# Second attention of a gated cross-attention block: where the softmax sums are inverted and how the values leave PSUM

## The reference, cut to what matters

```
q = LN(x) @ Wq.T + bq ; k, v = ctx @ Wk.T + bk, ctx @ Wv.T + bv      # 16 heads of 16
p = exp(clip(masked(q k / 4)))                                       # 16 x 128 x 128
attn = softmax over the context rows = p / sum(p)
delta = clip(residual_scale) * (concat_heads(attn @ v) @ Wo.T + bo)
x += tanh(g) * (LN(delta) * gamma + beta)
```

## Time and profile before

| | |
|---|---|
| median of 3 runs | 263.72 us (263.62 to 264.2) |
| profiled execution | 264.11 us, span 262.3 us |
| busy, share of the span | PE 81%, VectorE 69%, ScalarE 51%, GpSimd 32% |
| stage C, first product OT to last | 138.63 us to 190.57 us |
| granted TensorE clock, mean | 0.946 of full speed |

### The profile page before, as it was taken

The page is one execution under the profiler, slowest core; times in us unless marked ns, Lnnn a source line. Parts: engine busy times, 40 slices in busy tenths (PEclk is TensorE's granted clock), DMA queues, the critical chain, the costliest instruction groups (busy, mean ns, idle before and its releaser), DMA issues.

```text
span 262.3 us, 4538 instructions
## 1 busy us (share of the span) xinstructions
PE 212.0 (81%) x1658; PEld 174.5 (67%) x1658; DVE 181.0 (69%) x457; ACT 132.8 (51%) x296; POOL 83.9 (32%) x108
## 2 busy tenths in 40 slices
PE   0285557979889889897798688775999999999992
PEld 0264325858778778786576466654877888888882
DVE  2769879598988988786428999998984333262333
ACT  1138874478667667679755455553322323222220
POOL 2301111175856856868505333442100000000000
PEclk9999955699999999999959999997999999999999
DMA  5999003900000000000000000000000000020002
GB/s 169 369 390 301 5 0 139 343 1 0 2 0 0 2 1 0 2 2 0 0 2 2 0 2 4 0 4 0 2 2 0 0 0 2 0 80 2 0 0 80
DMA packets 9238, 12.55 MB, mean 48 GB/s; under 512 B 1025, under 2 KB 7937, under 8 KB 9217
## 3 DMA queue, kind: packets, MB, share of 16 engines
q1 hardware_dynamic: 8784, 12.07, 13.3%
q10 hardware_dynamic: 432, 0.20, 0.4%
HBM read 11.22 MB, written 1.05 MB: 47 GB/s over the span
## 4 chain that ended last, share of the span: by engine, by line
PE 50%; DVE 27%; ACT 7%; DMA 6%; issue 4%; POOL 3%; SPq 1%; DVEq 0%; ACTq 0%; POOLq 0%
PE PB L1259 16%; PE PB L1278 7%; DMA WRAW<-w_dram 6%; PE PB L1073 6%; PE PB L1172 4%; PE PB L1085 3%; DVE XV L524 3%; PE PB L1108 2%; PE PB L1112 2%; DVE HBQ L742 2%; PE PB L1019 2%; DVE RD L728 2%; DVE HBQ L572 2%; ACT SIL L906 2%; DVE HSD L578 2%
## 5 line engine op out<-in xcount | busy, mean ns | idle before, releaser
L1259 PE MATMUL PB<-SGN,WHI 128*128 128x512 f32 x128 | 40.5, 397 | 0.0
L1073 PE MATMUL PB<-SGN,XQH 128*128 128x512 f32 x64 | 27.7, 433 | 1.3 <-DVE XQL L553 1.3
L699 DVE TENSOR_TENSOR WRAW<-WRAW,PB 128x512 f32<-128x512 f32 x16 | 11.0, 686 | 24.0 <-ACT WRAW L993 23.9
L1278 PE MATMUL PB<-WHI,SGN 128*128 128x256 f32 x128 | 25.6, 283 | 2.2 <-DVE SGN L707 1.8
L1073 PE MATMUL PB<-SGN,XQL 128*128 128x512 f32 x64 | 27.1, 424 | 0.0
L289 POOL TENSOR_TENSOR RSTD<-MVS,MHALF 128x1 f32<-128x1 f32 x24 | 13.4, 560 | 40.9 <-DVE MVS L401 40.9
L1259 PEld LDWEIGHTS PB<-SGN,WHI 128*128 128x128 f32 x128 | 22.9, 188 | 4.5 <-issue 0.2
L1259 PE MATMUL PB<-SGN,WLO 128*128 128x512 f32 x64 | 25.2, 394 | 0.0
L993 ACT ACTIVATE WRAW<-PB 128x512 f32<-128x512 f32 x16 | 9.6, 600 | 28.0 <-PE PB L1259 28.0
L1278 PEld LDWEIGHTS PB<-WHI,SGN 128*128 128x128 f32 x128 | 20.7, 188 | 3.6 <-DVE SGN L707 2.4
L316 POOL TENSOR_TENSOR HBQ<-HBQ,HR 128x512 f32<-128x512 f32 x16 | 17.6, 1098 | 17.2 <-DVE HR L590 17.2
(11 more groups left out here) (122 smaller groups left out, 545.7 us busy)
## 6 DMA issues: line engine op xcount, KB each, us to landing
WRAW<-w_dram SPq DMA_DIRECT2D x2, 2048.0 KB, 12.1
X<-x_dram SPq DMA_DIRECT2D x2, 512.0 KB, 5.8
CTXT<-ctxt_dram SPq DMA_DIRECT2D x1, 1024.0 KB, 9.6
CTX<-ctx_dram SPq DMA_DIRECT2D x1, 1024.0 KB, 12.0
WRAW<-w_dram SPq DMA_DIRECT2D x1, 1024.0 KB, 14.9
WQK<-wqkvo_dram SPq DMA_DIRECT2D x1, 1024.0 KB, 7.8
WRAW<-wd_dram SPq DMA_DIRECT2D x1, 1024.0 KB, 10.1
out_dram<-X SPq DMA_DIRECT2D x4, 256.0 KB, 2.2
```

What stands on the lines that cost most here:

```text
L1073: mm = nc.tensor.matmul(PB[2 * half + m][:], part[:, p, c, :], sgn(m, c, a, b), start=(c == 0 and k == 0), stop=(c == DC - 1 and k == 1))
L1259: mm = nc.tensor.matmul(PB[2 * b + m][:], wcol(w_part, m, c, j), act_part[:, c, g * TG:(g + 1) * TG], start=(c == 0 and i == 0), stop=(c = ...
L1278: mm = nc.tensor.matmul(down_bank(g, k), act_part[:, b, ts], wdown(w_part, j), start=(j == 0 and i == 0 and k % 2 == 0), stop=(j == FC - 1 ...
```

## The change

The sums are no longer copied to 16 rows. A stationary block `SEL` (128 x 32, one column of ones) selects a row for each (feature half c, parity e, query half); 32 matmuls of 64 query columns place the 16 x 128 sums on 32 of the 128 rows of a 64-column block, and the reciprocal works on 64 columns. Four matmuls with a zero-one matrix `SPREAD` (128 x 128, built on GpSimd from the identity early in the program) spread the reciprocals to 256 columns of PSUM bank 7. ScalarE copies the values from bank 6 to SBUF (`PV`), and the product OT reads `PV` and the spread reciprocals.

With it the order changes. On TensorE: q(t+1), sums(t-1), values(t-1), spread(t-1), scores(t+1), transpose of t+2, transpose for stage D of t-3, delta(t-1). On VectorE: `norm_d(t-3)` stands before the product OT, `lo_d(t-3)` between the clamp and DL. On ScalarE: `q_out(t+1)`, the copy of the values, the exponentials of t+1 in two pairs with `copy_ht(t+2)` and `hi_d(t-3)` between; the four exponentials of tile 0 come before the loop. Stage D's preparation lags one tile more; its banks change (`down_bank`), and the wait of the first `down_d` for the last DL goes.

```diff
 # setup
-        ONE2 = sb("ONE2", [P, 2, HB32])
+        SEL = sb("SEL", [P, 2 * CT4, HB32])
+        SPREAD = sb("SPREAD", [P, 2 * DC, P])
-        RD = sb("RD", [P, D])
+        RD = sb("RD", [P, P // 2])
+        PV = sb("PV", [P, D])
-            return PB[(4, 6)[g % 2] + k // 2][:, (k % 2) * D:(k % 2 + 1) * D]
+            return PB[((4, 7), (5, 6))[g % 2][k // 2]][:, (k % 2) * D:(k % 2 + 1) * D]
 # GpSimd
+            for r in range(2 * CT4):
+                nc.gpsimd.memset(SEL[:, r, r:r + 1], 1.0).then_inc(set_pool, 1)
+            nc.gpsimd.memset(SEL[:, 0, 2 * CT4:], 1.0).then_inc(set_pool, 1)
+            for c in range(DC):
+                for half in range(2):
+                    nc.gpsimd.tensor_copy(SPREAD[:, 2 * c + half, :] ..., rows...)
 # VectorE step_c
+                if t == NT:
+                    gu_d(0)
                 if live(t - 1):
                     dve.wait_ge(c_dn, t)
-                    nc.vector.reciprocal(RD[:], PB[7][:, 0:D]).then_inc(c_rd, 1)
+                    nc.vector.reciprocal(RD[:], PB[7][:, 0:P // 2]).then_inc(c_rd, 1)
                 if live(t + 2):
                     norm(t + 2, p, 2)
+                if live(t - 3):
+                    norm_d(t - 3)
+                if t == NT:
+                    lo_gu(0)
                 if live(t - 1):
-                    dve.wait_ge(c_rd, t)
-                    dve.wait_ge(c_pv, t)
-                    need(dve, c_dl, t - 1)
-                    nc.vector.tensor_tensor(OT[:], PB[6][:, 0:D], RD[:], ALU.mult
+                    dve.wait_ge(c_sp, t)
+                    dve.wait_ge(c_pc, t)
+                    nc.vector.tensor_tensor(OT[:], PV[:], PB[7][:, D:2 * D], ALU.mult
-                if live(t - 2):
-                    norm_d(t - 2)
                 ...                       # the clamp
+                if live(t - 3):
+                    lo_d(t - 3)
                 if t == NT:
-                    gu_d(0)
-                    lo_gu(0)
+                    gu_d(1)
                 ...                       # DL and its statistics
-                if live(t - 2):
-                    lo_d(t - 2)
 # ScalarE step_c
+            def values_out(u):
+                act.wait_ge(c_pv, u + 1)
+                need(act, c_o, u)
+                nc.scalar.copy(PV[:], PB[6][:, 0:D]).then_inc(c_pc, 1)
             def step_c(t, p):
-                if live(t):
-                    exp_c(t, p, 0)
-                    exp_c(t, p, 1)
                 if live(t + 1):
                     q_out(t + 1)
-                if live(t):
-                    exp_c(t, p, 2)
-                    exp_c(t, p, 3)
+                if live(t - 1):
+                    values_out(t - 1)
+                if live(t + 1):
+                    exp_c(t + 1, 1 - p, 0)
+                    exp_c(t + 1, 1 - p, 1)
                 if live(t + 2):
                     copy_ht(t + 2, p, 4, xt_done, c_q, c_ht, 2 * NT)
-                if live(t - 2):
-                    hi_d(t - 2)
+                if live(t - 3):
+                    hi_d(t - 3)
+                if live(t + 1):
+                    exp_c(t + 1, 1 - p, 2)
+                    exp_c(t + 1, 1 - p, 3)
 # TensorE
+            def head_sums(u, p):
+                pe.wait_ge(c_p, u + 1)
+                for c in range(DC):
+                    for e in range(2):
+                        for half in range(2):
+                            r = (2 * c + e) * 2 + half
+                            for j in range(CT4):
+                                at = head_at(HPC * c + 2 * j + e) + half * (P // 2)
+                                mm = nc.tensor.matmul(
+                                    PB[7][HB32 * j:HB32 * (j + 1), 0:P // 2], SEL[:, r, :],
+                                    PR[:, p, at:at + P // 2], start=(r == 0),
+                                    stop=(r == 2 * CT4 - 1))
+                mm.then_inc(c_dn, 1)
+            def spread_sums(u):
+                pe.wait_ge(c_rd, u + 1)
+                for k in range(2 * DC):
+                    at = D + k * (P // 2)
+                    mm = nc.tensor.matmul(PB[7][:, at:at + P // 2], SPREAD[:, k, :], RD[:],
+                                          start=True, stop=True)
+                mm.then_inc(c_sp, 1)
             def step_c(t, p):
                 if live(t + 1):
                     q(t + 1, 1 - p)
                 if t == NT:
                     pe.wait_ge(c_ex, 4 * NT)
                     gate_up_d(0)
                 if live(t - 1):
-                    ...heads(7, lambda h: ONE2[:, h % 2, :], 1 - p).then_inc(c_dn, 1)
-                    ...heads(6, lambda h: V1[:, 1 - p, h, :], 1 - p).then_inc(c_pv, 1)
+                    head_sums(t - 1, 1 - p)
+                    head_values(t - 1, 1 - p)
+                if live(t - 1):
+                    spread_sums(t - 1)
                 if live(t + 1):
                     scores(t + 1, 1 - p)
                 if live(t + 2):
                     xt_c(t + 2, p)
+                if live(t - 3):
+                    xd_t(t - 3)
                 if t == NT:
                     gate_up_d(1)
                 if live(t - 1):
-                    ...                   # delta, then the transpose for stage D of tile t - 2
+                    delta(t - 1)
             def down_d(n):
-                if n == 0:
-                    pe.wait_ge(c_de, NT)
```

More of the change, by code:

```diff
@@ L298, in _ @@
                                         ).then_inc(rstd_ready, 1)
+            pool.wait_ge(ld["ident"], 16)
+            for c in range(DC):
+                for half in range(2):
+                    at = 4 * c + half
+                    rows = ident[:].rearrange("p (j s) -> p j s", s=HB32)[:, :, at:at + 3:2]
+                    nc.gpsimd.tensor_copy(
+                        SPREAD[:, 2 * c + half, :].rearrange("p (j e d) -> p j e d", e=2, d=HD),
+                        rows.unsqueeze(3).broadcast_to([P, CT4, 2, HD])).then_inc(set_spread, 1)
             for t in range(NT):
@@ L772, in step_c @@
                     stats(t - 1, 1 - p, t - 1 + 2 * NT)
-            pipeline(step_c, lag=1)
+                if t == NT:
+                    lo_gu(1)
+            for t in range(NT + 1):
+                step_c(t, t % 2)
             def update_d(g):
@@ L786, in update_d @@
                         in1=X[:, t, :], op0=ALU.mult, op1=ALU.add).then_inc(x_done, 1)
-            gu_d(1)
-            lo_gu(1)
-            norm_d(NT - 1)
             for n in range(2, NG * FC):
                 gu_d(n)
+                if n in (2, 4):
+                    norm_d(NT - 3 + n // 2)
+                if n in (3, 5):
+                    lo_d(NT - 3 + n // 2)
                 lo_gu(n)
-                if n == 2:
-                    lo_d(NT - 1)
                 if n >= FC and n % FC == 1:
@@ L967, in exp_c @@
                                      scale=1.0 / math.sqrt(HD)).then_inc(c_ex, 1)
+            def values_out(u):
+                act.wait_ge(c_pv, u + 1)
+                need(act, c_o, u)
+                nc.scalar.copy(PV[:], PB[6][:, 0:D]).then_inc(c_pc, 1)
             def step_c(t, p):
-                if live(t):
-                    exp_c(t, p, 0)
-                    exp_c(t, p, 1)
                 if live(t + 1):
                     q_out(t + 1)
-                if live(t):
-                    exp_c(t, p, 2)
-                    exp_c(t, p, 3)
+                if live(t - 1):
[3 more added lines that the diff above has]
+                    exp_c(t + 1, 1 - p, 1)
                 if live(t + 2):
                     copy_ht(t + 2, p, 4, xt_done, c_q, c_ht, 2 * NT)
-                if live(t - 2):
-                    hi_d(t - 2)
+                if live(t - 3):
[3 more added lines that the diff above has]
+                    exp_c(t + 1, 1 - p, 3)
             warm(ACT.Exp)
             copy_ht(1, 1, 4, xt_done, c_q, c_ht, 2 * NT)
+            for b in range(4):
+                exp_c(0, 0, b)
             pipeline(step_c, lag=0)
@@ L999, in _ @@
             warm(ACT.Silu)
[L1000 to L1005, removed]
+            for n in range(NG * FC):
+                if n in (3, 5):
+                    hi_d(NT - 3 + n // 2)
                 silu_d(n)
                 hi_gu(n)
-                if n == 2:
-                    hi_d(NT - 1)
+                if n == 0:
+                    values_out(NT - 1)
+                    hi_d(NT - 3)
         @block.tensor
@@ L1163, in q, with head_values @@
                 mm.then_inc(c_q, 1)
-            def heads(bank, parts, p):
+            def head_sums(u, p):
[11 more added lines that the diff above has]
+                mm.then_inc(c_dn, 1)
+            def head_values(u, p):
+                pe.wait_ge(c_v, 2 * u + 2)
+                need(pe, c_pc, u)
+                need(pe, d_hl, u - 2)
                 for c in range(DC):
@@ L1172, in heads, with delta, xd_t @@
                             mm = nc.tensor.matmul(
```

(27 more changed lines are left out.)

36 lines of the change are left out of this document (13 added, 23 removed).

## The result

The kernel after takes 270.36 us as a median of four runs (269.11 to 271.17), against 263.96 for the kernel before; the ratio is 1.0226, with an interval of 1.0193 to 1.0259. The change makes the kernel slower, as forecast, but by 6.4 us and not by 1.6, and the time lies outside the range. The profiled execution took 269.77 us, its span is 268.0 us (262.3 before).

A forecast was written before the change was run, and what follows sets the result against it. VectorE's list was taken to bound a stage C tile at 7.20 us. Start -1.9, rounds +2.2 and end +1.3 gave +1.6, 265.3 us as a median; range 261.6 to 267.0, the forecast's own 264.3 to 266.3.

The forecast's parts named there:

- start: Up to OT of tile 1: earlier tile 0 exponentials, earlier q(2), shorter reciprocal and perhaps an earlier clock return; -1.9 us.
- OT of tile 1 to OT of tile 6: Stage C's middle rounds: 38.58 us against 36.40 before, cost +2.2; nothing with a spread of 0.45.
- end: Last step, TensorE sets the time: sums +0.87, spread +0.88, first `down_d` wait -0.45; cost +1.3 us.
- the new loop: Stage C tile: spread, scores, transposes, delta, DL, statistics, reciprocal follow one another; 7.87 us a tile against 7.20.
- first scores bank about 0.9: In the `hi_d` route to DL: own estimate for the first scores bank, within the stream's 1.15 us.
- the clock, a rival: TensorE idling about 0.8 us a tile brings a fall to 1.2 GHz: up to +1.7, 267.0 us; chance 0.12.
- 1.43 a tile was harmless: Argument against the clock rival: TensorE's idle 1.43 us a tile in the kernel before had done no harm.
- Sums: TensorE's sums, 32 matmuls of 64 columns: between 0.87 and 1.74 us, taken at 1.74, hidden except at the end.
- the rival of cheap small matmuls: TensorE's spread and sums: time goes by columns, spread 0.45 and sums 0.87; put at 261.8 us, chance 0.27.
- Cancelled: Rival: `hi_d` isn't the last wait (-0.8) and the last step's sums are cheap (-0.87); 263.6 us, chance 0.15.

The follow-up runs named there:

- the kernel with ten fill products: Kernel after plus unread identity matmuls where TensorE waits for the reciprocal: three products at t = 2, six per later tile, ten in the last step; 267.8 us, ratio 1.0131.
- the one with two spreads: Kernel after with the eight spread instructions issued a second time, with the same results; 280.3 us, ratio 1.0639.

## Why the prediction was right or wrong

The span grew by 5.7 us and the forecast was 1.6. By the forecast's own three terms: start -1.32 for -1.9 (OT of tile 1 at 145.36, and 146.68 in the earlier trace rows); OT of tile 1 to OT of tile 6 42.24 us for 38.58; end +1.18 for +1.3 (268.0 - 187.60, and 262.3 - 183.08). So the middle term holds 3.66 of the 4.1 us that were missed.

**The mechanism was right.** "Spread, scores, transposes, delta, DL, statistics and reciprocal follow one another": the chain shows it, taking the scores out of it gives 5.6 us back, and putting them behind the reciprocal in the kernel before costs 2.8.

**The step that failed in size is the round of "the new loop".** For a full round at full clock:

| part of the loop | forecast | measured |
|---|---|---|
| spread and change of shape | 0.88 + 0.14 | 1.03 (160.09 to 161.12) |
| scores' start to DL, by `hi_d` | 2.87 | 3.16 (161.12 to 164.28) |
| DL to reciprocal | 3.37 | 3.51 (164.28 to 167.79) |
| reciprocal and hand-over | 0.61 | 0.60 (167.79 to 168.39) |
| round | 7.87 | 8.30 |

The second row holds the estimate "first scores bank about 0.9". A bank is complete only with the second half of the stream, and by the timeline the first exponential starts 1.16 us after the scores, with the stream's end: 0.26 too little. The other 0.14 is in DL to reciprocal, which had been copied from the earlier trace rows: there `lo_d` stood between DL and X, beside GpSimd's inverse root. Moved away, it leaves only D2 beside the root, the root takes 0.72 us (0.55 before), and X waits 0.50. With `lo_d` put back behind the statistics the root is 0.55 and DL to reciprocal 3.38. So `lo_d` had been cover for the root where it stood; the forecast moved it and kept the old length of the stretch that it left. Three full rounds at 0.43 make 1.29 us, the first round 7.57 for 7.37 makes 0.20, the last one 8.03 for 7.60 (its length at full clock, from the kernel with ten fill products) makes 0.43.

**The other part is the clock, a rival with a chance of 0.12.** It was priced as one fall of up to 1.7. The fourth and fifth rounds took 9.42 and 8.65 us where they take 8.30 and 8.03 at full clock: 1.74 us in the profiled execution, by two falls. TensorE's timeline in the second one:

```profile
178.84 1.15 PE L1253 MATMUL PB<-QM,MASKS 32*128 32x256 f32 x16
...
180.40 1.91 PE L1230 MATMUL PB<-WQK,OT 128*128 128x256 f32 x4
182.24 1.57 PE L1197 MATMUL PB<-HBQ,SEL 128*32 128x64 f32 x64
```

Delta takes 1.91 us, and 1.03 at full clock. The case was argued as an alternative to the forecast, with "1.43 a tile was harmless" against it; it is an addition to it. The idle time of a round was forecast at 0.8 us and is 1.64, because the loop is longer and the sums cheaper than forecast. The sum is 0.20 + 1.29 + 0.43 + 1.74 = 3.66.

**Sums:** taken at 1.74 us, measured 0.92. Columns count here, not instructions: 64 columns take half the time of 128 (27.2 ns in the earlier trace rows). The view of the sums' line, its weight loads (least, median, most ns), answers to the earlier trace rows:

```profile
L1197 PEld LDWEIGHTS PB<-HBQ,SEL x512: 106/110/178, 134.1 to 192.8; 128*32 128x32 f32 x171
```

64 instructions in 0.91 to 0.92 us are 14.3 ns from start to start, though each has a weight load of 110 ns: these overlap one another. This is against the sentence of the Trainium skill that the prediction weighed ("TensorE: Matmul & The Clock Gate", section "Wait — 56ns, not 53.3ns?"), by which starts are never closer than about 25 ns; the measurement decides. The spread has 128 weight columns and took 0.94 us (194.18 to 195.12) for the 0.88 forecast, so the rival of cheap small matmuls was half right, in the half that hardly counts: the sums are beside the chain, except in the last step.

**Start:** OT of tile 1 came at 145.36, just inside the forecast's 144.3 to 145.4, and partly by luck. The exponentials of tile 0 do come early, and q(2) starts at 132.12 (132.72 in the earlier trace rows): 0.60 earlier where 1.2 was forecast, 0.34 of the rest because stage C itself began later (scores(0) at 125.14, and 124.80 in the earlier trace rows). What made up for it is the clock, which came back a stage sooner. The values of tile 0, first before, then after:

```profile
136.43 1.94 PE L1172 MATMUL PB<-HBQ,V 128*32 128x128 f32 x32
135.68 1.05 PE L1211 MATMUL PB<-HBQ,V 128*32 128x128 f32 x32
```

From their start to that of the next stream it was 1.87 us (to 138.30) and is 0.98 (to 136.66), so 0.89 of the 1.32 came by it. The spread took most of that back, DL of tile 0 is 0.76 earlier (140.11, and 140.87 in the earlier trace rows), and the shorter reciprocal gives the remaining 0.56. The forecast had 1.3 without the clock and 2.2 with it.

**End:** right in its sum, not in its parts. The sums cost nothing there (0.91 us, and 0.90 before), the wait of the first `down_d` is gone as forecast, and the spread took 0.94 us behind a wait of 0.27. Not in the forecast: two tiles' transposes stand in stage D (205.34 and 214.51) where it was one, and TensorE waits 0.33 us for the second. The rest was not separated.

**"Cancelled"** fell with the first of its two conditions: `hi_d` is the last wait, 1.10 us ahead of `lo_d`. The second, cheap sums in the last step, came true.

## What to carry to other kernels

On an engine that works in order, an operation put behind a wait takes everything after it along; before moving one, list what stands behind it and ask whether the answer to the wait depends on any of it. Relieving the fullest engine pays only if the new operations don't close a loop through it and another engine: here, the same operations in another order make the difference between 2.3% slower and 1.4% faster (ratio 0.9863). The sign of such a loop in a profile is a round in which no engine is full and each waits for the next; and the idle time that it makes can cost a second time, through TensorE's clock.

## What the runs showed of the hardware

- Matmuls of 128 x 32 weights and 64 columns on four column groups start 14.3 ns apart (64 in 0.91 to 0.92 us), with 128 columns 27.2 ns apart; with 128 x 128 weights and 64 columns it is about 0.118 us (8 in 0.94).
- GpSimd's inverse root on 128 x 1 takes 0.55 us when VectorE runs `lo_d` beside it, and 0.72 in the tiles in which D2 stands there, in the same execution.
- In the kernel after the clock fell behind waits of TensorE of 1.64 and 1.36 us, and in two executions it stayed full in the rounds in which unread matmuls filled such waits. What exactly brings a fall is open: in the kernel after, one wait of 1.64 us was followed by full clock before the next was followed by a fall; the one with two spreads fell in the full rounds behind waits of 0.91, 1.36, 1.36 and 1.35; and the one with `lo_d` moved ran rounds with 0.99 without a fall until the last tiles. Executions of one kernel differ in it: of the kernel after, the one of 271.17 us has a mean clock of 0.930, the one of 269.11 has 0.949.
